# A four-layer kernel on one core: a 32 KB ring of bias rows with masks one pair later in layer 2, and two queries per step in the projection

## What is computed

```
xn = ln(x, g); q = xn @ Wq (16 heads); k, v = xn @ Wkv (one head)
q, k = l2norm(q) * q_scale, l2norm(k) * k_scale     # layers 1 and 3 only
sim = q @ k.T * scale + bias; causal; softmax over [null, keys]; out = attn @ v
x = x + ln(out @ Wout, g_out)
```

## Time and profile before

| what | value |
|---|---|
| three runs | 2519.36, 2514.55, 2511.8 us; median 2514.55 us |
| the profiled execution | 2516.95 us, its span 2514.8 us |
| mean granted clock of PE | 0.907 |
| busy share of the span | PE 81%, DVE 70%, ACT 53%, POOL 46% |
| bytes moved by DMA | 322.41 MB, mean 128 GB/s |
| layer 1: project's products, attend (first logits to last output) | 322 to 417 us, 455 to 925 us |
| layer 2: project, attend | 1030 to 1097 us, 1104 to 1660 us |
| layer 3: project's products, attend, end of close | 1844 to 1938 us, 1976 to 2437 us, 2515 us |

### The profile page before, as it was taken

How to read it: one execution, slowest core, us unless ns; L and a number is a source line. 1 busy time by engine, 2 the same in 40 slices (tenths; PEclk the granted TensorE clock), 3 DMA queues, 4 the chain that set the end, 5 groups by cost and what they waited for, 6 DMA issues and landing times. The chain is left out here.

```text
span 2514.8 us, 46901 instructions
## 1 busy us (share of the span) xinstructions
PE 2031.9 (81%) x11738; PEld 1439.0 (57%) x11738; DVE 1753.7 (70%) x4112; ACT 1335.7 (53%) x2872; POOL 1144.4 (46%) x1544
## 2 busy tenths in 40 slices
PE   6993287799999988678888888885277699999988
PEld 5883254566666657465555556554155466666657
DVE  5877855688878855656666666646946688887865
ACT  2221255577766653355566556542245577777753
POOL 1221104566766632026666666622103566666642
PEclk8997588899999999789998999997588799999999
DMA  2001046433333331476676666641045543333323
GB/s 72 25 14 39 3 166 216 153 106 113 101 119 116 101 110 62 165 257 185 207 210 200 197 197 198 195 168 39 1 135 192 184 127 100 116 103 112 122 93 109
DMA packets 171006, 322.41 MB, mean 128 GB/s; under 512 B 22838, under 2 KB 51132, under 8 KB 170844
## 3 DMA queue, kind: packets, MB, share of 16 engines
q1 hardware_dynamic: 170844, 320.59, 40.7%
HBM read 242.76 MB, written 94.52 MB: 134 GB/s over the span
## 5 line engine op out<-in xcount | busy, mean ns | idle before, releaser
L1358 POOL TENSOR_SCALAR at_row<-at_row,at_inv 128x129 f32<-128x129 f32 (+7 forms) x384 | 725.3, 1889 | 306.4 <-DVE at_inv L1515 303.9
L1562 ACT ACTIVATE at_row<-at_row,at_nmax 128x129 f32<-128x129 f32 (+7 forms) x768 | 595.2, 775 | 217.4 <-DVE at_nmax L1534 214.5
L1534 DVE CUSTOM_DVE_ANT_0 at_row<-at_s,bias,at_row 128x128 f32<-128x128 f32 (+7 forms) x768 | 623.2, 811 | 109.5 <-PE at_s L1462 50.8
L1474 PE MATMUL at_t<-ident,at_row 128*128 128x128 f32 x3456 | 551.1, 288 | 113.5 <-POOL at_row L1358 81.4
L1474 PEld LDWEIGHTS at_t<-ident,at_row 128*128 128x128 f32 x3456 | 400.6, 145 | 312.8 <-POOL at_row L1358 145.7
L1461 PE MATMUL at_s<-k_hh,q_hl 128*128 128x512 f32 (+3 forms) x1152 | 466.7, 405 | 48.3 <-SPq L1424 32.0
L1490 PE MATMUL at_o<-at_pt,v 128*64 128x512 f32 (+3 forms) x2304 | 443.5, 508 | 7.9 <-ACT at_pt L1555 6.2
L1555 ACT ACTIVATE at_pt<-at_t 128x512 f32<-128x512 f32 (+2 forms) x576 | 309.0, 536 | 226.0 <-PE at_t L1474 219.6
L1373 DVE COPY at_pt<-at_t 128x128 f32<-128x128 f32 (+3 forms) x576 | 278.9, 484 | 194.6 <-PE at_t L1474 193.2
L1462 PE MATMUL at_s<-k_lp,q_h 65*128 65x512 f32 (+3 forms) x1152 | 395.9, 356 | 0.0
L1461 PEld LDWEIGHTS at_s<-k_hh,q_hl 128*128 128x128 f32 x1152 | 228.4, 198 | 89.9 <-SPq L1424 33.4
(11 more groups left out here) (223 smaller groups left out, 3088.4 us busy)
## 6 DMA issues: line engine op xcount, KB each, us to landing
q_hl<-q_dram SPq DMA_DIRECT2D x192, 256.0 KB, 4.4
bias<-bands_dram SPq DMA_DIRECT2D x64, 512.0 KB, 5.6
q_dram<-pj_qh SPq DMA_DIRECT2D x96, 256.0 KB, 2.4
q_dram<-pj_ql SPq DMA_DIRECT2D x96, 256.0 KB, 2.3
q_h<-q_dram SPq DMA_DIRECT2D x96, 256.0 KB, 5.1
o_dram<-at_o_sb SPq DMA_DIRECT2D x96, 256.0 KB, 4.5
o_in<-o_dram SPq DMA_DIRECT2D x12, 2048.0 KB, 8.8
bands_dram<-brow_dram SPq DMA_DIRECT2D x2, 8192.0 KB, 32.6
```

Source lines behind the costliest of these rows:

```text
L1358: return eng.tensor_scalar(cells, cells, inv[:, i:i + 1], None, ALU.mult)
L1474: last = eng.transpose(t_ps[m % NTR][:, c * P:(c + 1) * P], row[:, u % RING, here:here + P], t["ident"][:])
L1534: eng.tensor_tensor_reduce(out=row[:, u % RING, ZERO:ZERO + width], in0=s_ps[u % 2][:, 0:width], in1=bt[:, lo:lo + width], scale=-1.0, sca ...
L1562: eng.activation(cells, cells, ACT.Exp, scale=-1.0, bias=nmax[:, i:i + 1], accum_out=rsum[:, i:i + 1]).then_inc(s["exp"], 1)
```

## The change

Five edits. (A) In layer 2 the ring of bias rows has 32 KB per partition, 16 blocks in flight and 12 loaded in project; layers 1 and 3 keep 16 KB. (B) POOL masks two units in each odd step, behind the scaling and the null columns, units n+3 and n+4. (C) In the normed projection the spread, scaling and the two halves are done for two queries in a step, from R_AT = 14 on; qn has 4 places in place of 2, qs 12 in place of 14, and the low halves are shared out differently between DVE and POOL. (D) The first bias tiles are issued at SP's 10th query, in all layers. (E) o_in is two tiles, and in layer 2 the first lies in the ring's second half; so SP waits for the last unit's addition before `load_outputs(..., 0)`, in all three layers.

```diff
--- before.py
+++ after.py
@@ -30,12 +30,16 @@
+HEAD_SLOTS, BIAS_IN_FLIGHT, ROWS_FIRST = 4, 16, 12
+ROW_SPACE = 8 * S
+
+
 def bias_places():
...
     for width in widths:
-        at = 0 if at + width > 4 * S else at
+        at = 0 if at + width > ROW_SPACE else at
         places.append(at)
@@ -46,7 +50,6 @@
-HEAD_SLOTS, BIAS_IN_FLIGHT = 4, 8
 BIAS_AT, BIAS_AFTER = bias_places()
@@ -848,10 +851,10 @@
     N = NCH * ITEMS
-    NQS, NMP, NQN, NST = 14, 3, 2, 4
-    R_LAG = 15 if normed else 0
-    HI_LAG = R_LAG + 2 if normed else 1
-    FIRST = HEAD_SLOTS if bias is None else BIAS_IN_FLIGHT
+    NQS, NMP, NQN, NST = 12, 3, 4, 4
+    R_AT = 14
+    LAST = N + 12
+    FIRST = HEAD_SLOTS if bias is None else ROWS_FIRST
     names = ["dve", "var", "std", "xn", "xtr", "xt_hi", "xt_lo", "main", "sq", "ss", "norm", "inv", "inv_t",
@@ -899,7 +902,16 @@
         def low_by_vector(q):
-            return not normed or (q >= (NCH - 1) * NPAIR and q % 2 == 1)
+            return not normed or q % 8 in (1, 4, 6) or q == NCH * NPAIR - 1
+
+        def due(step, first):
+
+            after = step - first
+            if not normed:
+                return [(after // ITEMS, after % ITEMS)] if 0 <= after < N else []
+            found = [(after // ITEMS - back, 2 * (after % ITEMS + back * ITEMS) + n) for back in range(2) for n in range(2)]
+            found = [(c, r) for c, r in found if 0 <= c < NCH and r < ITEMS - 1]
+            return [(c, r if r == KEY else r + 1) for c, r in found]
@@ -935,7 +947,7 @@
                         load_queries(eng, t, s["first"], g, 0)
-                    if q == 3 * NPAIR - 1:
+                    if q == NPAIR + 1:
                         if bias is None:
@@ -994,10 +1006,8 @@
-                def spread(g):
-                    c, i, q = item(g)
-                    if i == VALUE:
-                        return
+                def spread(c, i):
+                    q = c * NPAIR + i - 2
                     r = r_number(c, i)
@@ -1007,7 +1017,7 @@
                 x_transposes(0)
-                for g in range(N + R_LAG):
+                for g in range(N + (R_AT - ITEMS + ITEMS // 2 + 1 if normed else 0)):
                     if chunk(g, 8) is not None and chunk(g, 8) + 1 < NCH:
@@ -1022,8 +1032,8 @@
                         sums(chunk(g, 11), True)
-                    if g >= R_LAG:
-                        spread(g - R_LAG)
+                    for c, i in due(g, R_AT):
+                        spread(c, i)
@@ -1098,7 +1108,7 @@
                 x_high(0)
-                for g in range(1, N + HI_LAG):
+                for g in range(1, LAST):
                     if chunk(g, 2) is not None and chunk(g, 2) + 1 < NCH:
@@ -1115,12 +1125,11 @@
                         values_out(chunk(g, 4))
-                    if HI_LAG <= g < N + HI_LAG:
-                        c, i, q = item(g - HI_LAG)
+                    for c, i in due(g, R_AT + 2 if normed else 1):
                         if i == KEY:
...
                         elif i != VALUE:
-                            query_high(c, i, q)
+                            query_high(c, i, c * NPAIR + i - 2)
@@ -1232,25 +1241,23 @@
                 x_low(0)
-                for g in range(1, N + HI_LAG + 2):
+                for g in range(1, LAST):
                     if chunk(g, 4) is not None:
...
                         inverse(chunk(g, 12))
-                    if normed and R_LAG < g <= N + R_LAG:
-                        c, i, q = item(g - R_LAG - 1)
+                    for c, i in due(g, R_AT + 1) if normed else ():
                         if i == KEY:
                             key_norms(c)
-                        elif i != VALUE:
-                            query_norms(c, i, q)
+                        else:
+                            query_norms(c, i, c * NPAIR + i - 2)
                     if chunk(g, 9) is not None and chunk(g, 9) + 1 < NCH:
                         x_low(chunk(g, 9) + 1)
-                    if HI_LAG <= g < N + HI_LAG:
-                        c, i, q = item(g - HI_LAG)
+                    for c, i in due(g, R_AT + 2 if normed else 1):
                         if i == KEY:
                             key_low(c)
-                        elif i != VALUE and low_by_vector(q):
-                            query_low(c, i, q)
+                        elif i != VALUE and low_by_vector(c * NPAIR + i - 2):
+                            query_low(c, i, c * NPAIR + i - 2)
                     if chunk(g, 1) is not None and chunk(g, 1) + 1 < NCH:
@@ -1295,7 +1302,7 @@
     pairs = slice(c // 2 * NPAIR, (c // 2 + 1) * NPAIR)
-    eng.dma_start(t["o_in"][:, c % 2, :, :], t["o_dram"][pairs, :, cols].rearrange("a p i -> p a i")).then_inc(sem, 16)
+    eng.dma_start(t["o_in"][c % 2], t["o_dram"][pairs, :, cols].rearrange("a p i -> p a i")).then_inc(sem, 16)
@@ -1400,7 +1407,7 @@
                 def row_bias(place, ready, n):
-                    if ready and n < NBIAS:
+                    if ready and n < ROWS_FIRST:
                         return
@@ -1422,7 +1429,7 @@
                     eng.sem_inc(s[f"q{g}"], 48)
-                for n in range(NBIAS):
+                for n in range(HEAD_SLOTS if toeplitz else ROWS_FIRST):
                     eng.sem_inc(s[f"bias{n}"], 16)
@@ -1433,6 +1440,7 @@
                     eng.wait_ge(s[f"o{g}"], 8 * NGRP * TURNS * (B - 1) + 16)
+                place(B - 1, TURNS - 1).wait(eng, "biased", U)
                 load_outputs(eng, t, s["first"], 0)
@@ -1628,8 +1636,6 @@
                 def step(turn, n, has):
-                    if not toeplitz and has(n + 4, U):
-                        mask_corner(turn, n + 4)
                     if turn.known() and 0 <= turn.turn < TURNS and turn.half < B - 1 and n % 6 == 2 and 14 <= n < 38:
@@ -1639,6 +1645,9 @@
                         null_logits(turn, n + 5)
+                    for u in (n + 3, n + 4):
+                        if not toeplitz and has(u, U):
+                            mask_corner(turn, u)
@@ -1666,7 +1675,7 @@
             def o(n):
-                return t["o_in"][:, n // CT % 2, :, (n % CT) * P:(n % CT + 1) * P]
+                return t["o_in"][n // CT % 2][:, :, (n % CT) * P:(n % CT + 1) * P]
@@ -1859,7 +1868,7 @@
                 t["q_h1"] = sbl("q_h1", [P, 2, 2, BANK], FR)
-                t["bias"] = sbl("bias", [P, HEAD_SLOTS * S])
+                t["bias"] = sbl("bias", [P, HEAD_SLOTS * S if normed else ROW_SPACE])
                 with tensors(nc) as (sbp, _):
@@ -1870,8 +1879,10 @@
                     t[f"wo_{part}"] = sbl(f"wo_{part}", [P, NPAIR, D], FR)
-                t["o_in"] = sbl("o_in", [P, 2, NPAIR, BANK])
-                t["wo_raw"] = t["o_in"][:, 1, :, 0:D]
+                t["o_in"] = [sbl("o_in0", [P, NPAIR, BANK])[:] if normed else
+                             t["bias"][:, ROW_SPACE - NPAIR * BANK:].rearrange("p (a i) -> p a i", a=NPAIR),
+                             sbl("o_in1", [P, NPAIR, BANK])[:]]
+                t["wo_raw"] = t["o_in"][1][:, :, 0:D]
                 attend(nc, t, w, bias)
...
```

## The result

The changed kernel takes 2547.35 us (median of four runs, 2540.33 to 2553.35) beside 2513.18 for the kernel before (2506.56 to 2519.36): the ratio is 1.0135, 95% interval 1.0094 to 1.0177. It is 34 us slower, where 20 us faster was forecast. The profiled executions have spans of 2514.8 and 2550.0 us, and the 35 us between them can be laid out by stages.

| stage | before, us | after, us | difference | forecast |
|---|---|---|---|---|
| projection, layer 1 | 132.6 | 127.2 | -5.4 | -12 |
| projection, layer 2 | 72.0 | 77.9 | +5.9 | +2 |
| projection, layer 3 | 132.1 | 122.8 | -9.3 | -12 |
| attend, layer 1 | 457.9 | 453.4 | -4.5 | 0 |
| attend, layer 2 | 539.4 | 553.5 | +14.1 | -21 |

What follows compares the result with a forecast made beforehand. PE was taken to bound layers 1 and 3, waits for late bias blocks to slow layer 2. Terms -24 + 3 + 18 + 5 + 2 - 24 = -20 us gave 2494 against the median 2514.55; forecast range 2480 to 2508.

Steps and rivals of the forecast that it cites:

- 104.0 us of waiting for blocks: Layer 2's attend: POOL's 66 waits for bias blocks before masking, expected to fall under 15 us with 16 blocks in flight.
- the loop: Layer 2's attend: moved masks close a ring over each pair through POOL and DVE, 32.4 us a run before an addition.
- The first rival: Layer 2's attend: the mask loop does not bind, some 28.9 us a run, kernel 2433 us; chance 0.12.
- I add 0.3 and take 32.7: Layer 2's attend: 0.3 us on the 32.4 sum for slower PE places; 34.2 to 32.7 a run, -24 us in all.
- the scalings: Loop term in layer 2: POOL's scalings at the layer's mean of 1.83 us, 14.6 us for a run's 8 pairs.
- fixed part: Loop term in layer 2: gaps between inverse, scaling, mask and addition plus the mask, 8 x 1.48 = 11.8 us a run.
- additions: Loop term in layer 2: DVE's bias additions at 0.74 us each, 5.9 us a run.
- the second rival: Layer 2's attend: the mask loop costs more than the wait it replaces; 2531 us at 35.0 a run; chance 0.15.
- Start of each turn: Layer 2's attend: early units' blocks are issued late, 8 turns x 0.4 = +3 us (0 to 12, or 15).
- The tail: End of attend: last stores queue behind the load of o_in; +9 in layers 1 and 3 each, +5 in layer 2.
- The projection: Normed layers 1 and 3, edits C and D: tail -12.5, steady part +0.5 or so; 12 us gained each, -24 together.
- the 12 blocks: Layer 2's projection: 2.7 MB loaded at the 10th query instead of 1.3 MB at the 24th, +2 us (0 to 5.6).

Runs made afterwards that it cites:

- e1: Changed kernel with edit B alone undone: POOL masks unit n+4 ahead of the scaling again; 2475.83 us beside 2510.74 for the kernel before.
- e7: Changed kernel with POOL's two masks between the scaling and the null columns; 2489.66 us beside 2512.11 for the kernel before.
- e8: Changed kernel with DVE scaling one cell per even row instead of the row (work left out); 2501.68 us beside 2512.11 for the kernel before.
- e4: Changed kernel with SP's wait for the last unit's addition before loading o_in kept in layer 2 alone; 2524.55 us beside 2510.74 for the kernel before.
- e6: Kernel of e5 with layer 2's first two last-turn output stores issued ahead of the o_in load, which waits for unit 29; ratio 0.9705 to the kernel before.
- e3: Kernel before with edit C alone (two queries per step in the normed projection); 2490.5 us beside 2510.74 for the kernel before.
- e5: Kernel of e1 with edit D undone and e4's wait in layer 2 alone; 2446.14 us beside 2512.11 for the kernel before.
- e9: Kernel of e6 with 8 bias blocks of layer 2 loaded in the projection instead of 12; 2429.92 us beside 2511.89 for the kernel before.
- e2: Kernel before with edit B alone (masks behind scaling and null columns, ring still 16 KB); 2522.16 us beside 2510.74 for the kernel before.

## Why the prediction was wrong

**The wait that goes, and what takes its place: right in kind.** The 104.0 us of waiting for blocks went whole, and the loop inverse, scaling, null copies, mask, addition came in its place, as the prediction drew it; e1 takes the mask out of it and e7 the two copies, and the time followed each time. The first rival (the loop does not bind) is out.

**Its price: wrong, and this is the step that failed.** "I add 0.3 and take 32.7" should have been 35.0. Two terms of that sum were too small: the scalings, and the 0.3 for pairs that do not close the loop. The terms measured in the changed kernel, as means by width over its 14 runs: fixed part 8 x 1.51 = 12.1 (11.8 in the sum), additions 5.9 (5.9), scalings 15.8 (14.6). That is 33.8 us. The scaling's mean was taken from a layer in which POOL came late, held up by masks, so that DVE had mostly scaled its row of the same width before: 10 of the 14 scalings of 128x897 took 2.53 us there, 11 of 128x769 2.21 and 13 of 128x641 1.89, which are the times of e8. In the loop both are released by the same inverse and start together in all 14 runs: 3.03, 2.6 and 2.2. e8 shows that this, and not DVE being busier in general, is the 0.3 to 0.5 us. The prediction weighed the Trainium skill (GPSIMD Engine Reference, "1. Specifications") on contention with VectorE and let it reach layer 1's mean at most; but layer 1's mean mixes two cases as well, as the next rows show. The trace agrees that the two contend; what was missing is the reading form by form and by what starts together.

In layer 1 of the kernel before, the two scalings of 128x897 start together in both of these places, first POOL and then DVE:

```profile
621.29 3.03 POOL L1358 TENSOR_SCALAR at_row<-at_row,at_inv 128x897 f32<-128x897 f32 x1 [0.40 <-DVE at_inv L1515]
621.33 0.68 DVE L1358 TENSOR_SCALAR at_row<-at_row,at_inv 128x897 f32<-128x897 f32 x1
...
766.17 2.54 POOL L1358 TENSOR_SCALAR at_row<-at_row,at_inv 128x897 f32<-128x897 f32 x1 [1.12 <-DVE at_inv L1515]
766.21 1.45 DVE L1358 TENSOR_SCALAR at_row<-at_row,at_inv 128x897 f32<-128x897 f32 x1
```

Either POOL pays half a microsecond or DVE pays 0.8. In the loop of layer 2 it was POOL, all 14 times.

The remaining 1.2 us (33.8 to 35.0) are mostly the two widths that do not always close the loop: the pairs of 385 took 4.4 us in the mean where their loop is 3.7, and those of 257 3.6 where it is 3.3; layer 1, bound by PE, takes 4.6 for 385. A pair costs the larger of the two, and a sum of either over all eight is too small. The prediction put 0.3 on this from one stretch of three pairs, whose sum hid the one of 385; that pair took 4.5 to 4.6 us in every run of the kernel before. So the forecast of -21 for layer 2's attend turned into +14 (32.7 against 34.2 us a run became 35.0 against 34.5), and the second rival came about. Its price per pair was the right thing to ask for, and its chance of 0.15 too low for a margin of 0.21 us a pair. At 35.0 us a run it gave 2531; most of the other 16 us are the projections, 13 short of the forecast.

**Start of each turn.** No cost seen, where +3 was forecast: POOL waits for no block in the window, and the seven runs that begin a turn take 34.7 us in the mean (34.1 to 36.3), the seven between them 35.2 (34.3 to 36.1). But the layer's very first run, 25.8 before, is 31.1, by the loop.

**The tail.** +8.3, +5.4 and +10.4 for +9, +5 and +9. Right in size, and partly by luck: the prediction took the 8 us from the last stores that end attend, and the 7.93 us fell ahead of the third output's copy, which needs the place of the first of the four stores, as e4 and e6 show.

**The projection.** C alone gives -12.3 and -11.5 (e3; -11 and -11.7 in the mean of the kernels without D), the -12 that was forecast for both. That the number fits is luck: from the last product to the first logits e3 saves 9.6 and 8.6 us, where -12.5 was forecast, and up to the last product it saves 2.7 and 3.0, where +0.5 was. D was costed at about 2 us in the steady part and costs 4.2 and 2.9. ACT's waits for stores in layer 1's projection are 10.7 us in the changed kernel beside 4.8 before and 5.8 in e5, half of them at one stroke (the 5.41 us); in layer 2 the 12 blocks cost 4.4 (e9 beside e6) and their earlier place 1.2 more, for +2.

**What stays open.** Attend in layers 1 and 3 moved by -4.5 and +7.0 without an edit that touches their steady state. Kernels with edit C (e8, which leaves work out, aside) have 448 to 453 us in layer 1 (before and e2: 458 and 456) and 453 to 457 in layer 3 (449 and 447), whatever else they change, so it is tied to when the phase begins or what is in flight then. The traces show what goes with it. A run there takes 27 to 32 us at a granted clock of 1.00, and nearly always how long it takes follows which engine paid in the scalings of 769 and 897. In layers 1 and 3 of all kernels but e8, 13 runs each (the 8th has other work on POOL), a run in which POOL paid both times took 28.1 us in the mean (171 runs), one in which DVE paid at 897 alone 28.9 (33), at 769 alone 29.7 (13), at both 30.6 (43). Two runs of layer 1 before, of the first and the last kind:

```profile
595.59:623.46 27.87, 26.88 (x167) 17.83 (x167) 22.74 (x62) 20.42 (x47) 17.53 (x24) 1.00 0.35 106
738.58:769.12 30.54, 28.03 (x173) 18.34 (x171) 24.44 (x62) 20.20 (x47) 18.75 (x26) 1.00 0.38 114
```

DVE paid at 769 in 4 runs of layer 1 before and in 2 after, in none of layer 3 before and in 4 after, which is the sign and about the size of the -4.5 and +7.0. It is not the whole cause: in e8, without DVE's scaling, four runs still take 29.1 to 29.4 us and most 27.1 to 27.8. What decides who pays is open. At 769 DVE's scaling started 0.04 us or more ahead of POOL's where POOL paid and 0.07 or 0.08 behind it where DVE did, but at 897 it started 0.03 to 0.04 us behind nearly always, whoever paid.

## What to carry to other kernels

Before an instruction is moved behind another on an in-order engine, follow the ring from it back to itself through all engines and add it up once per trip; a wait that vanishes says nothing if the ring is as long. Take each duration of that sum in the company that it will have: an operation that is released together with its neighbour on the other engine is not the operation that came late and ran alone. And put the item that the ring needs first right behind the operation that feeds it: two small copies and their wait, behind the masks instead of ahead, were worth 58 us.

## What was not expected of the hardware

Where POOL and DVE start to scale rows of the same width together, one of the two takes longer. In layers 1 and 3 of all kernels but e8, at 128x897, either POOL takes 3.0 us and DVE 0.7 (198 times) or POOL 2.5 and DVE 1.2 to 1.5 (82 times); at 128x769 it is 2.6 and 0.6 (204 times) or 2.2 and 1.2 (56 times). At 128x641 POOL paid nearly always: 2.2 us, where e8 has 1.89. At 128x1025 POOL's 2.9 us are the same in e8 and it is DVE that pays: 1.49 us in the loop, and 0.74 to 0.81 in 10 of 15 places of layer 2 before, where POOL was at another row or at its copies. In layer 2's loop POOL paid at 641, 769 and 897 every time, by 0.33 to 0.5 us, though DVE's instruction lasts only 0.5 to 0.7.
